# The shared expert's halves run beside routing and beside the scan, and the out projection shares the down product's accumulation

## Chip, cores and metric

The program runs on one core of a Trainium2 chip. The metric is the device time of one execution in microseconds (us), as the median of several runs. Engines are called PE or TensorE (matrix products), DVE or VectorE, ACT or ScalarE, POOL or GpSimd, and SP, which here only issues DMAs. Each has its own queue and works through it in order; they meet by semaphores.

## What is computed

T = 8192 rows (2 sequences of 4096) of H = 1024 values. Each row is normalised, a small state-space branch (D = 96 channels, N = 16 states) and a mixture of experts run on the normalised rows, and all is added up:

```python
xn = _layernorm(x)
x = x + attn(xn) + ffn(xn)
# attn: z = layer_norm(xn, w, b) @ in_proj.T      (1024 -> 96)
#       u = silu(conv3(z)); delta = softplus(...) * 0.001
#       state = exp(delta*A) * state + delta*B*u ; y = C . state + u*D
#       out = y @ out_proj.T + xn                 (96 -> 1024)
# ffn:  router: sigmoid scores, 4 of 8 groups, 8 of 32 experts, weights * 2.5
#       routed = sum over the 8 of w * (silu(x@Wg) * (x@Wu)) @ Wd   (inner 512)
#       shared = silu(x@Sg) * (x@Su) @ Sd                           (inner 1024)
```

## The kernel before

It has four stages, each a block in which all engines start together and end together.

**route_stage** (L64 to L533) takes 16 chunks of C = 512 rows, each J = 4 tiles of 128. `norms` on DVE makes `xn` for four tiles in one go, with the power -1/2 from POOL; POOL adds `bs = xt + xn`; SP stores xn and bs. PE turns xn (`transposes`, into `tp`) and multiplies it with the router's and the projection's weights (`project`, into `lg`). `route` on DVE picks the experts of a chunk and computes for each row and expert the slot in a table; slots and weights (`payload`) stay in SBUF for all rows. The 96 projected channels stay in SBUF as `zT`.

**scan_stage** (L536 to L922) takes the same 16 chunks. Channels times states make 1536 lines, in NG = 12 groups of 128. For each group PE spreads delta and delta*u (`spread_to`, four products into `rep_d` and `rep_u`), ACT takes the exponential (`dA`), DVE multiplies (`dBu`) and runs the recurrence (`hs`, L884), POOL multiplies with C (`hc`, L669) and PE collects (`collect`, into `yp`, a float32 product). `rep_d`, `rep_u` and `op` have two buffers each. Eight half tiles of the out projection (`out_half`, L758) run in groups 3 to 10 of the next chunk; DVE adds them to the base rows that SP has loaded (`add_half`, L871), and SP stores them as output.

**plan_stage** (L935 to L1054) counts the rows of each expert, lists the tiles, and meanwhile loads the first weights and gathers the first rows.

**expert_stage** (L1057 on) runs 656 tiles of 128 rows through one half expert of inner width 512 each: first SH * T / P = 128 tiles of the shared expert (two halves, 64 tiles each), then 528 of the routed experts. Every float32 operand is split into a high and a low part (type fp32r), and each product is three products:

```python
m(dst, hi, whi[:, cols], start=begin, stop=False)              # L1409
m(dst, hi, wlo[:, cols], start=False, stop=False)              # L1410
return m(dst, lo, whi[:, cols], start=False, stop=end)         # L1411
```

PE's order in a tile t is: gate (24 products, into `pg`), up (24, into `pu`), turning the rows of t+1 (8, into `tx`), the down product of t-1 (24, into `pd`), turning the activated tile (4, into `ta`, L1445). ACT makes the high parts and Silu, DVE the low parts (L1321 for weights, L1332, L1337), `av = pu * sg` (L1370) and the scaled result (L1344). POOL gathers the rows by table and adds results to the output by indirect DMAs. While the first 64 tiles run, POOL also writes the table of slots: eight indirect DMAs of 128 entries in each tile (`scatter`, L1200).

## Time and profile before

| | us |
|---|---|
| median of 3 runs | 13304.63 |
| lowest, highest | 13290.81, 13305.15 |
| profiled execution, device time | 13301.22 |
| its span in the trace | 13299.4 |
| TensorE busy in it | 12585.9 (95%) |
| VectorE, ScalarE, GpSimd busy | 4435.6, 2255.9, 2837.1 |

The span is what the trace covers; it lies 1.8 us under the device time of the same execution. A busy TensorE is not one at its peak: its ends are modelled, so a product's cost is read from one start to the next. The columns of a timeline row are start, duration, engine, line, operation, tile written <- tiles read, shape and count, and in brackets the idle time just before with what ended it.

### The profile page before, as it was taken

How to read it: one execution, taken by the hardware profiler on the slowest of the kernel's cores; microseconds unless marked ns; L12 is line 12 of the kernel's file. 1: busy time of each engine (PE TensorE's matmuls, PEld its weight loads, DVE VectorE, ACT ScalarE, POOL GpSimd, SP SyncE). 2: the span in 40 equal slices, each digit the busy share in tenths (PEclk: the TensorE clock that was granted, in tenths of full speed). 3: DMA queues.
4: the chain of work that ended last, by engine and by line, in shares of the span. 5: the costliest groups of instructions: out<-in, count | busy, mean ns of one | idle time of the engine just before them, and what ended most of it. 6: DMA issues, size and time to landing. Idle time of an engine off the chain costs nothing.

```text
span 13299.4 us, 218878 instructions
## 1 busy us (share of the span) xinstructions
PE 12585.9 (95%) x58520; PEld 10224.2 (77%) x58521; DVE 4435.6 (33%) x6772; ACT 2255.9 (17%) x3430; POOL 2837.1 (21%) x2929
## 2 busy tenths in 40 slices
PE   4377799999999999999999999999999999999998
PEld 3333488888888888888888888888888788888887
DVE  8887622222222222222332223223233323222222
ACT  1133211111111111111111112111112212111111
POOL 3222266621111111111111111111111111111111
PEclk7688899999999999999999999999999999999999
DMA  4312222232232332333332324323334434223322
GB/s 187 136 63 76 87 61 60 60 78 59 59 78 60 78 79 59 77 60 79 96 98 59 79 59 110 65 60 96 79 96 115 113 79 115 59 60 71 66 59 53
DMA packets 376393, 1057.82 MB, mean 80 GB/s; under 512 B 142082, under 2 KB 142530, under 8 KB 352552
## 3 DMA queue, kind: packets, MB, share of 16 engines
q0 software_dynamic: 205600, 689.56, 24.9%
q1 hardware_dynamic: 170760, 367.91, 7.5%
q14 instruction: 23, 0.19, 0.0%
q8 instruction: 10, 0.16, 0.0%
HBM read 608.87 MB, written 448.41 MB: 79 GB/s over the span
## 4 chain that ended last, share of the span: by engine, by line
PE 86%; DMA 1%; DVE 0%; issue 0%; ACT 0%; DVEq 0%; SPq 0%; ACTq 0%; POOL 0%; POOLq 0%
PE pg L1409 9%; PE pg L1411 9%; PE pd L1411 9%; PE pd L1410 9%; PE pg L1410 9%; PE pd L1409 9%; PE pu L1411 9%; PE pu L1410 9%; PE pu L1409 9%; PE tx L1404 4%; PE ta L1445 2%; DMA stage<-in_w_all 0%; DVE w_lo L1321 0%; ACT w_hi L1255 0%; DVEq L1054 0%
## 5 line engine op out<-in xcount | busy, mean ns | idle before, releaser
L1370 DVE TENSOR_TENSOR av<-pu,sg 128x512 f32<-128x512 f32 x656 | 453.8, 692 | 5681.0 <-PE pu L1411 5504.9
L1409 PE MATMUL pg<-w_hi,x_hi 128*128 128x512 f32 x5248 | 2113.7, 403 | 13.0 <-DVE x_lo L1332 13.0
L1409 PE MATMUL pd<-w_hi,a_hi 128*128 128x512 f32 x5248 | 2098.2, 400 | 8.1 <-DVEq L1356 8.0
L1411 PE MATMUL pd<-w_hi,a_lo 128*128 128x512 f32 x5248 | 2057.6, 392 | 0.0
L1411 PE MATMUL pg<-w_hi,x_lo 128*128 128x512 f32 x5248 | 2054.6, 392 | 0.0
L1410 PE MATMUL pd<-w_lo,a_hi 128*128 128x512 f32 x5248 | 2053.5, 391 | 0.0
L1410 PE MATMUL pg<-w_lo,x_hi 128*128 128x512 f32 x5248 | 2046.2, 390 | 0.0
L1411 PE MATMUL pu<-w_hi,x_lo 128*128 128x512 f32 x5248 | 2043.5, 389 | 0.0
L1409 PE MATMUL pu<-w_hi,x_hi 128*128 128x512 f32 x5248 | 2041.5, 389 | 0.0
L1410 PE MATMUL pu<-w_lo,x_hi 128*128 128x512 f32 x5248 | 2041.5, 389 | 0.0
L1214 POOL DMA_INDIRECT out_rows<-y,idx_s x656 | 1046.9, 1596 | 4266.2 <-DVE y L1344 4116.2
L1344 DVE TENSOR_SCALAR y<-pd,idx_s 128x512 f32<-128x512 f32 x1312 | 982.0, 751 | 1946.4 <-PE pd L1411 1901.4
L1259 ACT ACTIVATE x_hi<-tx 128x512 fp32r<-128x512 f32 x1314 | 720.9, 595 | 3437.5 <-PE tx L1404 3274.6
L1411 PEld LDWEIGHTS pg<-w_hi,x_lo 128*128 128x128 f32 x5248 | 985.6, 188 | 220.5
L1411 PEld LDWEIGHTS pd<-w_hi,a_lo 128*128 128x128 f32 x5248 | 985.4, 188 | 206.7
L1410 PEld LDWEIGHTS pu<-w_lo,x_hi 128*128 128x128 f32 x5248 | 985.3, 188 | 204.3
L1411 PEld LDWEIGHTS pu<-w_hi,x_lo 128*128 128x128 f32 x5248 | 985.3, 188 | 204.3
L1409 PEld LDWEIGHTS pu<-w_hi,x_hi 128*128 128x128 f32 x5248 | 985.3, 188 | 204.3
L1409 PEld LDWEIGHTS pd<-w_hi,a_hi 128*128 128x128 f32 x5248 | 987.9, 188 | 199.1 <-issue 9.5
L1409 PEld LDWEIGHTS pg<-w_hi,x_hi 128*128 128x128 f32 x5248 | 987.2, 188 | 199.6 <-DVE x_lo L1332 12.4
L1410 PEld LDWEIGHTS pg<-w_lo,x_hi 128*128 128x128 f32 x5248 | 989.6, 189 | 190.5
L1410 PEld LDWEIGHTS pd<-w_lo,a_hi 128*128 128x128 f32 x5248 | 988.3, 188 | 192.1
(227 smaller groups left out, 10228.4 us busy)
## 6 DMA issues: line engine op xcount, KB each, us to landing
stage<-in_w_all SPq DMA_DIRECT2D x186, 1024.0 KB, 9.3
xt<-in_x SPq DMA_DIRECT2D x16, 2048.0 KB, 12.9
xn_rows<-xn SPq DMA_DIRECT2D x16, 2048.0 KB, 6.7
base_rows<-bs SPq DMA_DIRECT2D x16, 2048.0 KB, 8.4
base<-base_rows SPq DMA_DIRECT2D x64, 512.0 KB, 5.6
out_rows<-base SPq DMA_DIRECT2D x64, 512.0 KB, 2.7
idx_g<-slot_table SPq DMA_DIRECT2D x658, 1.0 KB, 1.7
xraw<-xn_rows,idx_g POOLq DMA_INDIRECT x658
```

The lines of the kernel that those rows point to most:

```text
L1214: g.indirect_dma_start(out=out, out_offset=bass.IndirectOffsetOnAxis(ap=idx_s[q][:, 0:1], axis=0), in_=y[q][:], in_offset=None, compute_op ...
L1259: a.activation(x_hi[q][:, 4 * h:4 * h + 4], tx[h][:], ACT.Copy).then_inc(xh_ready, 1)
L1344: v.tensor_scalar(y[q][:, h * 512:(h + 1) * 512], pd[h][:], idx_s[q][:, 1:2].bitcast(F32), None, ALU.mult).then_inc(y_ready, 1)
L1370: v.tensor_tensor(av[:], pu[:], sg[:], ALU.mult).then_inc(av_ready, 1)
L1404: last = nc.tensor.transpose(tx[h][:, k], xraw[q][:, (4 * h + k) * P:(4 * h + k + 1) * P], ident[:])
L1409: m(dst, hi, whi[:, cols], start=begin, stop=False)
L1410: m(dst, hi, wlo[:, cols], start=False, stop=False)
L1411: return m(dst, lo, whi[:, cols], start=False, stop=end)
L1445: last = nc.tensor.transpose(ta[:, i], av[:, i * P:(i + 1) * P], ident[:])
```

## The change

The shared expert leaves the expert stage; that one now runs the 528 routed tiles alone, with its own first loads and gathers, which no longer lie in the plan stage.

In routing, the work goes tile by tile, no longer in chunks of four. The first half of the shared expert (6 weight chunks, each as high and low part in SBUF) runs on each tile. The rows that are turned for the router also feed the high and low parts, `sx_hi` and `sx_lo`, which are stored for the next stage. The result is added to the base rows (`summed`), which go to the output at once. `pd` is the pair `pg, pu`: the down product of t-1 overwrites the gate of t once Silu has read it. `route` is cut into four parts, one per tile. The projected channels go to memory (`z_d`) and come back in the scan. The scatters to the table are done here by POOL, eight per tile, the last 48 in the scan.

In the scan, the second half of the shared expert runs on the tiles of the chunk before. Its turned parts are loaded again by POOL's queue. PE's work of one group, a `slot`, stands after gate, after up and after down. The out projection of a half tile is accumulated onto its down product, and one addition puts both onto the output rows, which SP loads and stores. `rep_d` and `rep_u` have one buffer each, `hc` is split into two fp32r parts by ACT and DVE for the collection. Chunk 0 has no FFN; there its weights come in. The last chunk's FFN follows the scan.

The diff, cut to the order of the work (added lines; the removed ones are the loops described above; first the helpers, then GpSimd, TensorE and VectorE in routing, then TensorE and VectorE in the scan):

```diff
+def product(nc, dst, hi, lo, whi, wlo, cols, begin, end):
+    m = nc.tensor.matmul
+    m(dst, hi, whi[:, cols], start=begin, stop=False)
+    m(dst, hi, wlo[:, cols], start=False, stop=False)
+    return m(dst, lo, whi[:, cols], start=False, stop=end)
+def gate_or_up(nc, dst, xh, xl, w_hi, w_lo, base):
+    for k in range(KH):
+        n, c = base + k // 4, k % 4 * I
+        last = product(nc, dst, xh[:, k], xl[:, k], w_hi[n], w_lo[n], slice(c, c + I), k == 0, k == KH - 1)
+    return last
+def down_half(nc, dst, a_hi, a_lo, w_hi, w_lo, h, end=True):
+    for i in range(KI):
+        n, c = 4 + i // 2, i % 2 * H + h * 512
+        last = product(nc, dst, a_hi[:, i], a_lo[:, i], w_hi[n], w_lo[n], slice(c, c + 512), i == 0,
+                       end and i == KI - 1)
+    return last
...
+            def scatter(c, r, part):
+                wait_apart(pool, pool_passed, slots_ready, c + 1)
+                for n in range(part * K, part * K + K):
+                    g.indirect_dma_start(
+                        out=table, out_offset=bass.IndirectOffsetOnAxis(ap=slots[r][:, n:n + 1], axis=0),
+                        in_=payload[r][:, n], in_offset=None).then_inc(scattered[r], 16)
+            def chunk(c, r):
+                for k in range(J):
+                    if not ends(c, k, 1):
+                        base(*later(c, k, 1))
+                    if not ends(c, k, 2):
+                        cc, kk = later(c, k, 2)
+                        power(cc, kk)
+                        power2(cc, kk, r if k < 2 else 1 - r)
+                    if k and not (known(c, 0) or known(c, 1)):
+                        scatter(c - 2, r, k - 1)
+                    if not k and not (known(c, 0) or known(c, 1) or known(c, 2)):
+                        scatter(c - 3, 1 - r, 3)
...
+            def down(c, k):
+                t = c * J + k
+                pe.wait_ge(al_ready, t)
+                for h in range(2):
+                    if not ends(c, k, 0):
+                        pe.wait_ge((sg_ready, av_ready)[h], t + 1)
+                    down_half(nc, pd[h][:], a_hi, a_lo, w_hi, w_lo, h).then_inc(down_done, 1)
+            def chunk(c, r):
+                for k in range(J):
+                    t = c * J + k
+                    begun = not (known(c, 0) and k == 0)
+                    pe.wait_ge(xl_ready, t * 2 + 2)
+                    if not begun:
+                        pe.wait_ge(split_lo, 2)
+                    if not (known(c, 0) and k < 2):
+                        pe.wait_ge(y_ready, t * 2 - 3)
+                    gate_or_up(nc, pg[:], x_hi[k % 2], x_lo[k % 2], w_hi, w_lo, 0).then_inc(gate_done, 1)
+                    if not begun:
+                        pe.wait_ge(split_lo, 4)
+                    if not (known(c, 0) and k < 2):
+                        pe.wait_ge(y_ready, t * 2 - 2)
+                    gate_or_up(nc, pu[:], x_hi[k % 2], x_lo[k % 2], w_hi, w_lo, 2).then_inc(up_done, 1)
+                    if not ends(c, k, 1):
+                        turn_rows(*later(c, k, 1))
+                    if known(c, 0) and k == 1:
+                        pe.wait_ge(split_lo, 6)
+                    if begun:
+                        down(c, k)
+                    if not ends(c, k, 1):
+                        project(*later(c, k, 1), r if k < 3 else 1 - r)
+                    if k == 1 and not known(c, 0):
+                        z_turned(c - 1)
+                    if k == 3 and not known(c, 0):
+                        ranks(c - 1)
+                    pe.wait_ge(av_ready, t + 1)
+                    if not ends(c, k, 1):
+                        pe.wait_ge(xnT_ready, t * 2 + 3)
+                        pe.wait_ge(xl_ready, t * 2 + 3)
+                    for i in range(KI):
+                        last = nc.tensor.transpose(ta[:, i], sg[:, i * P:(i + 1) * P], ident[:])
+                    last.then_inc(ta_done, 1)
...
+            def chunk(c, r):
+                for k in range(J):
+                    t = c * J + k
+                    begun = not (known(c, 0) and k == 0)
+                    if begun:
+                        a_low(t - 1)
+                    if not ends(c, k, 2):
+                        norms(*later(c, k, 2), r if k < 2 else 1 - r)
+                    activated(t)
+                    if not ends(c, k, 1):
+                        x_low(*later(c, k, 1))
+                    if begun:
+                        summed(*later(c, k, -1))
+                    if k == 0 and not (known(c, 0) or known(c, 1)):
+                        route(c - 2, r, 3)
+                    if k < 3 and not known(c, 0):
+                        route(c - 1, 1 - r, k)
...
+            def slot(s, r, q):
+                if q + 1 < NG:
+                    spread_to(s, q + 1)
+                elif not last_of(s):
+                    spread_to(s + 1, 0)
+                if q:
+                    collect(s, r, q - 1)
...
+            def down_tile(t, chunk_done, j, y, end=False):
+                pe.wait_ge(al_ready, t + 1)
+                pe.wait_ge(y_ready, chunk_done)
+                for h in range(2):
+                    if not end:
+                        pe.wait_ge((sg_ready, av_ready)[h], t + 2)
+                    down_half(nc, pd[h][:], a_hi, a_lo, w_hi, w_lo, h, False)
+                    m(pd[h][:], y[:, j * P:(j + 1) * P], w_o[:, h * 512:(h + 1) * 512], start=False, stop=True)\
+                        .then_inc(down_done, 1)
+            def ffn_tile(mth, k, r, between):
+                t = mth * J + k
+                begun = not (known(mth, 0) and k < 2)
+                gate(t, k, begun)
+                between(0)
+                up(t, k, begun)
+                between(1)
+                if k:
+                    down_tile(t - 1, mth + 1, k - 1, yT[r])
+                elif not known(mth, 0):
+                    down_tile(t - 1, mth, J - 1, yT[1 - r])
+                between(2)
+                turn_activated(t)
...
+            def chunk(s, r):
+                for q in range(NG):
+                    k = q // 3
+                    t = s * J + (k - J)
+                    ffn = not known(s, 0)
+                    begun = ffn and not (known(s, 1) and k == 0)
+                    if q % 3 == 1 and ffn:
+                        activated(t)
+                    if q + 1 < NG:
+                        advance(s, r, q + 1)
+                    elif not last_of(s):
+                        if known(s, CPB - 1):
+                            dve.wait_ge(dA_free, CPB * NG)
+                            clear_state(2)
+                        advance(s + 1, 1 - r, 0)
+                    if not last_of(s):
+                        if q == 0:
+                            convolve(s + 1, 1 - r)
+                        if q == 5:
+                            bias_dt(s + 1)
+                        if 6 <= q < 10:
+                            softplus(s + 1, 1 - r, q - 6)
+                        if q == 10:
+                            lows(s + 1)
+                    if q == 1 and not known(s, 0):
+                        tail(s - 1, 1 - r)
+                    hc_low(s, q)
+                    if known(s, 0):
+                        weights_low(q)
+                    if q % 3 == 1 and begun:
+                        summed(t - 1, (k - 1) % J, 0)
+                    if q % 3 == 2 and begun:
+                        summed(t - 1, (k - 1) % J, 1)
+                    if q % 3 == 2 and ffn:
+                        a_low(t)
```

GpSimd's queue in routing, before: per chunk one power, four base sums, one power.

```order
23 L256 TENSOR_TENSOR rstd<-mv,minus_half 128x4
24 L258 ISA
25 L261 TENSOR_TENSOR bs<-xt,xn 128x1024
26 L258 REGISTER_ALU
27 L261 TENSOR_TENSOR bs<-xt,xn 128x1024
28 L258 REGISTER_ALU
29 L261 TENSOR_TENSOR bs<-xt,xn 128x1024
30 L258 REGISTER_ALU
31 L261 TENSOR_TENSOR bs<-xt,xn 128x1024
32 L264 TENSOR_TENSOR rs_0<-mv_0,minus_half 128x4
```

The same queue now, two tiles in the loop (`bases` is the base sum):

```order
104 L404 DMA slot_table<-payload,slots 262656x2 x8
105 L388 TENSOR_TENSOR bases<-xt,xn 128x1024
106 L391 REGISTER_ALU
107 L392 TENSOR_TENSOR rstd<-mv,minus_half 128x1
108 L396 TENSOR_TENSOR rs_1<-mv_1,minus_half 128x1
109 L404 DMA slot_table<-payload,slots 262656x2 x8
110 L388 TENSOR_TENSOR bases<-xt,xn 128x1024
```

Each tile has both powers, and eight scatters stand between them and the base sum.

TensorE's queue in the scan, before: one group, then a half of the out projection.

```order
317 L747 MATMUL rep_d<-d_hi,spread 128x512
318 L748 MATMUL rep_d<-d_lo,spread 128x512
319 L749 MATMUL rep_u<-du_hi,spread 128x512
320 L750 MATMUL rep_u<-du_lo,spread 128x512
321 L766 MATMUL yp<-hc,gather 96x512
322 L757 REGISTER_ALU
323 L758 MATMUL op<-w_o,yT 128x512
```

Now, from the end of a gate over one slot to the start of an up product (`tpg`, `tpu`, `tw_`, `tx_`: gate, up, weights and rows of the FFN in this stage):

```order
2374 L68 MATMUL tpg<-tw_hi,tx_lo 128x512
2375 L1210 ISA
2376 L1212 MATMUL rep_d<-d_hi,spread 128x512
2377 L1213 MATMUL rep_d<-d_lo,spread 128x512
2378 L1214 MATMUL rep_u<-du_hi,spread 128x512
2379 L1215 MATMUL rep_u<-du_lo,spread 128x512
2380 L1219 ISA
2381 L1222 MATMUL yp<-hc_hi,gather 96x512
2382 L1223 MATMUL yp<-hc_lo,gather 96x512
2383 L1256 REGISTER_ALU
2384 L66 MATMUL tpu<-tw_hi,tx_hi 128x512
```

A group's six products stand between blocks of 24, and the out projection has left this place.

VectorE's queue in routing now, the layer norm of one tile from its variance on, behind the low part of an activated tile and ahead of the product of gate and up (before, all four tiles of a chunk went through each of these steps together):

```order
156 L633 TENSOR_SCALAR mv<-mv 128x1
157 L634 REGISTER_ALU
158 L636 ISA
159 L637 REGISTER_ALU
160 L638 ISA
161 L639 TENSOR_SCALAR xn<-xt,mv,rstd 128x1024
162 L643 BN_STATS st<-xn 128x6 x2
163 L39 REGISTER_ALU
164 L645 BN_AGGR mv_0<-st 128x2
165 L56 REGISTER_ALU
166 L646 TENSOR_SCALAR mv_0<-mv_0 128x1
167 L673 TENSOR_TENSOR ssg<-spu,ssg 128x512
```

The product `ssg`, for which TensorE waits, stands behind the whole layer norm of a tile two ahead.

## Rows read from the trace of the kernel before

**Rows 1.** The page, the chain that ended last, shares of the span by engine.
```profile
PE 86%; DMA 1%; DVE 0%; issue 0%; ACT 0%; DVEq 0%; SPq 0%; ACTq 0%; POOL 0%; POOLq 0%
```
**Rows 2.** Busy by stage: length, PE, PEld, DVE, ACT, POOL, granted clock, DMA share, GB/s.
```profile
0.00:631.00 631.00, 260.22 (x1856) 235.35 (x1857) 564.12 (x1597) 90.49 (x196) 207.94 (x116) 0.70 0.44 166
631.00:1554.00 923.00, 681.67 (x1552) 317.03 (x1552) 711.85 (x1020) 312.44 (x422) 252.78 (x201) 0.83 0.19 73
1554.00:1593.00 39.00, 1.94 (x8) 1.57 (x8) 15.43 (x39) 9.56 (x7) 10.34 (x12) 0.50 0.53 202
1593.00:3862.00 2269.00, 2266.79 (x10730) 1883.74 (x10731) 559.84 (x775) 320.85 (x524) 873.75 (x1016) 1.00 0.29 64
3862.00:13262.00 9400.00, 9375.30 (x44376) 7786.55 (x44374) 2584.39 (x3345) 1522.52 (x2283) 1492.30 (x1586) 1.00 0.34 78
```
**Rows 3.** Timeline of the expert stage, a shared tile and the first routed gate.
```profile
2700.95 1.03 PE L1404 MATMUL tx<-ident,xraw 128*128 128x128 f32 x8
2701.21 0.69 DVE L1370 TENSOR_TENSOR av<-pu,sg 128x512 f32<-128x512 f32 x1 [9.28 <-PE pu L1411]
...
2713.21 0.39 PE L1409 MATMUL pu<-w_hi,x_hi 128*128 128x512 f32 x1
...
2718.66 1.03 PE L1404 MATMUL tx<-ident,xraw 128*128 128x128 f32 x8
...
3861.62 0.48 PE L1409 MATMUL pg<-w_hi,x_hi 128*128 128x512 f32 x1
```
**Rows 4.** Timeline of routing: layer norm, base sums, router's product, second part of routing.
```profile
27.57 7.06 DVE L421 TENSOR_SCALAR xn<-xt,mv,rstd 128x1024 f32<-128x1024 f32 x4 [1.17 <-POOL rstd L256]
28.47 10.71 POOL L261 TENSOR_TENSOR bs<-xt,xn 128x1024 f32<-128x1024 f32 x4 [0.93 <-DVE xn L421]
...
314.29 1.01 POOL L256 TENSOR_TENSOR rstd<-mv,minus_half 128x4 f32<-128x4 f32 x1 [22.99 <-DVE mv L415]
...
327.75 2.05 PE L340 MATMUL lg<-wcat,xnT 128*128 128x128 f32 x16 [0.74 <-ACT xnT L283]
...
332.29 0.09 DVE L463 MATCH_VALUE_LOAD gi<-g,gs 128x8 f32 x1
...
340.59 1.22 DVE L493 TENSOR_REDUCE w<-prod 128x32 f32<-128x1024 f32 x1
```
**Rows 5.** Timeline of the expert stage, scatters and a VectorE pass beside them.
```profile
2715.77 0.97 POOL L1200 DMA_INDIRECT slot_table<-payload_cur,slot_cur  x1 [0.30 <-issue]
2716.75 2.29 DVE L1321 TENSOR_TENSOR w_lo<-stage,w_hi 128x2048 fp32r<-128x2048 f32 x1 [7.50 <-ACT w_hi L1255]
2717.04 2.84 POOL L1200 DMA_INDIRECT slot_table<-payload_cur,slot_cur  x1 [0.30 <-issue]
```
**Rows 6.** Timeline of the scan.
```profile
671.14 1.28 DVE L884 TENSOR_TENSOR_SCAN hs<-dA,state,dBu 128x512 f32<-128x512 f32 x1
...
1308.74 0.77 PE L747 MATMUL rep_d<-d_hi,spread 96*128 96x512 f32 x1 [3.68 <-DVE dBu L880]
1309.30 0.63 PE L748 MATMUL rep_d<-d_lo,spread 96*128 96x512 f32 x1
1309.73 0.63 PE L749 MATMUL rep_u<-du_hi,spread 96*128 96x512 f32 x1
...
1320.31 1.28 ACT L712 ACT_TABLE_LOAD   x1
...
1322.81 1.02 PE L736 MATMUL op<-u,w_C 96*128 96x512 f32 x2
...
1323.89 0.39 PE L748 MATMUL rep_d<-d_lo,spread 96*128 96x512 f32 x1
```
**Rows 7.** Start of the expert stage; then the page's DMA issues (KB each, us to landing).
```profile
1580.61 7.31 ACT L1255 ACTIVATE w_hi<-stage 128x2048 fp32r<-128x2048 f32 x4 [57.82 <-PEq L943]
...
1593.37 0.80 PE L1409 MATMUL pg<-w_hi,x_hi 128*128 128x512 f32 x1 [10.80 <-DVE x_lo L1332]
...
stage<-in_w_all SPq DMA_DIRECT2D x186, 1024.0 KB, 9.3
```

More of the change, by code:

```diff
@@ L183, in route_stage, with chunks, known, ends @@
         block = ctx.enter_context(nc.Block())
+        def chunks(eng, chunk):
+            chunk(0, 0)
+            chunk(1, 1)
+            with eng.Fori(1, NC // 2 - 1) as i:
+                for r in range(2):
+                    chunk(i * 2 + r, r)
+            chunk(NC - 2, 0)
+            chunk(NC - 1, 1)
+        def known(c, n):
+            return isinstance(c, int) and c == n
+        def ends(c, k, d):
+            return isinstance(c, int) and c * J + k + d >= NT
         @block.sync
@@ new lines, in _ @@
+            for k in range(2):
+                power(0, k)
+                power2(0, k, 0)
+            base(0, 0)
+            pool.wait_ge(fills, FILLS)
+            chunk(0, 0)
+            chunk(1, 1)
+            chunk(2, 0)
+            chunk(3, 1)
+            with pool.Fori(2, NC // 2 - 1) as i:
+                for r in range(2):
+                    chunk(i * 2 + r, r)
+            chunk(NC - 2, 0)
+            chunk(NC - 1, 1)
+            scatter(NC - 3, 1, 3)
+            for part in range(J // 2):
+                scatter(NC - 2, 0, part)
@@ L311, in _ @@
+            for q in range(NCH):
+                act.wait_ge(staged[q % 2], q // 2 * 16 + 16)
+                a.activation(w_hi[q][:], stage[q % 2], ACT.Copy).then_inc(split_hi, 1)
+                if q == 1:
+                    x_high(0, 0)
+            chunks(act, chunk)
+            a_high(NT - 1)
+            z_row(NC - 1, 1)
         @block.tensor
@@ L379, in _ @@
+            turn_rows(0, 0)
+            project(0, 0, 0)
+            chunks(pe, chunk)
+            down(NC, 0)
+            z_turned(NC - 1)
+            ranks(NC - 1)
         @block.vector
@@ L553, in sem, with sems @@
             return ctx.enter_context(nc.semaphore(name))
+        def sems(name, n):
+            return [sem(f"{name}{i}") for i in range(n)]
+        w_hi = ring("tw_hi", [P, WC], F32R, NCH)
+        w_lo = ring("tw_lo", [P, WC], F32R, NCH)
+        x_hi = ring("tx_hi", [P, KH, P], F32R)
+        x_lo = ring("tx_lo", [P, KH, P], F32R)
+        sg = sb("tsg", [P, I])
+        a_hi = sb("ta_hi", [P, KI, P], F32R)
+        a_lo = sb("ta_lo", [P, KI, P], F32R)
+        sums = sb("sums", [P, 2, H])
+        bs = [sums[:, q] for q in range(2)]
+        ident = sb("tident", [P, P])
         cw = sb("cw", [D, 3])
@@ L671, in _ @@
+            chunks(pool, chunk, ((4, NC),))
+            for k in range(2):
+                t = NT - J + k
+                pool.wait_ge(up_done, t + 1)
+                load_x(t + 2, k)
+            pool.wait_ge(scattered, LEFT * 16)
         @block.scalar
@@ L1424, in down @@
                 for h in range(2):
[L1425 to L1429 removed]
+                    down_half(nc, pd[h][:], a_hi, a_lo, w_hi, w_lo, h).then_inc(down_done, 1)
             def tile(t, q):
```

1441 lines of the change are left out of this document (825 added, 616 removed).

## The prediction

> **What bounds the kernel now.** I read the chain that ended last first, then the stages. The chain is 86% TensorE, and waits for anything else are 1% or less [rows 1]. The stages say where that holds [rows 2]: routing (0 to 631) and scan (631 to 1554) keep TensorE busy for 260 of 631 and 682 of 923 us at a mean clock of 0.70 and 0.83, with VectorE at 564 and 712. The expert stage runs it without a hole at full clock: 2267 of 2269 us for the 128 shared tiles (1593 to 3862), 9375 of 9400 for the 528 routed ones. The last 37 us hold no work. So a tile in the expert stage costs what TensorE needs for it: 17.71 us from one turning of rows to the next [rows 3], of which 72 products are 72 x 0.227 = 16.35 (24 of them lie between 2713.21 and 2718.66, 5.45 us). Whoever moves 128 tiles under stages in which TensorE has holes saves the holes. The question is how much of 17.71 each tile costs there.
>
> **What goes.** The 128 shared tiles lie between the first gate product at 1593.37 [rows 7] and the first routed one at 3861.62 [rows 3]: 2268 us. From there the routed part is unchanged in its instructions; it lasts 13299.4 - 3861.6 = 9438 us, its closing loops included. Its first tile now starts without a predecessor's down product (5.5 us less) and at the low clock (some 4 more), so I keep 9436. The wait that SP gets there, for a gather issued two tiles ago, costs nothing: that gather had to land before the tile's own products.
>
> **The routing stage.** TensorE now has, per tile, what the expert tile has (17.71, the turned rows are shared with the router), and the router's product, 2.05 with its modelled end [rows 4]. That is 19.7 to 19.8. What must fit beside it:
> - VectorE had 564 us for 64 tiles, 8.8 each. The FFN adds six passes over 128x512 (av, two x_lo, a_lo, two sums) at 0.69 [rows 3]: 12.9 of 19.8. But it is not even: the second part of routing takes 8.3 (332.29 to 340.59) and falls in one tile of four. There it is 8.3 + 4.1 + the layer norm of one tile. Unbatched, that is two passes of statistics at 1.2, xn 0.9 (its start at 27.57 to Pool's at 28.47, when Pool is idle), Pool's power 1.0, and an estimated 2 for small operations and hand-overs: 6.3. Sum 18.7, and the chain has to come round before the second half of the down product, which waits for av. I take 1 us per chunk for it.
> - GpSimd gets a ring of its own. Per tile it does power, second power, eight scatters that stood in the expert stage before, and the base sum. VectorE's layer norm stands between the two powers. Scatters start 1.27 apart (2715.77, 2717.04) [rows 5], so 0.8 + 8 x 1.27 = 11.0; base 10.71 / 4 = 2.7; two powers 2.0; VectorE between them 3.1. Ring: 18.8. It fits under 19.8 by 1 us only.
> - The base rows no longer go to memory and come back; out, turned rows and rows are stored instead, about 2.5 MB per tile of 20 us, 125 GB/s. The stage moved 166 GB/s before [rows 2]. SP waits in order (base, xn, x_lo, sums); each is a tile old when needed. I cost it at nothing; if the stores came later than one tile, VectorE's xn would wait for them.
>
> So a tile costs 19.8 if all fits; I take 20.3, for the 1 us per chunk and some port trouble on Pool, and hold 22.5 as the upper bound (first rival). The start: six weight chunks pass two staging buffers, each 9.3 to land [rows 7], 1.8 for w_hi (7.31 / 4) [rows 7] and 2.3 for w_lo [rows 5]; three rounds of 13.4 after a first arrival near 24 (an estimate) end at 64, VectorE then owes the layer norm of tile 2 with Pool's base before it, and the gate of tile 1 starts at 76. 62 tiles of 20.3 lead to the last gate at 1335. Behind it: its own products 11, down product of the tile before 5.5, turning and its two parts 2.5, 18 of routing left to VectorE, and about 8 for sums, stores and the barrier: 45. **Routing ends at 1380**, against 631.
>
> **The scan stage.** A tile's blocks of 24 products now alternate with slots of the scan. Per tile: 16.35 + 0.35 for turning, three slots of six products of the same kind (four spreads and the collection as two parts), 18 x 0.227 = 4.1, two halves of the out projection accumulated onto the down product, and one of the four projections of a chunk. Those three are plain float32, two passes each; two passes and one single product lie between 1322.81 and 1323.89, 1.08, so 0.85 for one [rows 6]. Sum 23.4, with changes of mode 23.5: 94 us per chunk. Beside it VectorE has 712 / 16 = 44.5 per chunk, twelve low parts of hc at 0.69 and sixteen passes of the FFN at 0.69: 64. ScalarE 312 / 16 = 19.5, twelve high parts and eight FFN passes at an estimated 0.6 (w_hi's 2048 columns take 1.8, [rows 7]), and table loads, since each tile's Silu stands between exponentials: 2 x 1.28 [rows 6] per tile, about 42. Both fit. Single spread buffers make each slot wait for the exponential and product of the slot before, but a block of 5.45 lies between: after a gate, Silu with its load, the exponential with its load and the high part need about 4.5, the recurrence, state and low part end near 6.1, and TensorE comes for them at 5.45 + 1.4 + 0.9 = 7.7. With the convolution (2.7 more), the logarithms with their load and the last softplus part in front of the low part, it is late by about 1.1, 2.2 and 0.8. So 4 us per chunk, 98; bounds 94 and 106. The stage then is: 40 until the first recurrence (671 as before, [rows 6]) and 3 for new constants; chunk 0 without FFN, (923 - 40) / 16 = 55 plus twelve half w_lo at 1.15 and low parts at 0.69, 77; 15 x 98 = 1470; four tiles alone, (16.7 + 1.7 + 0.5) x 4 = 76; the last down product and store 14. Sum 1680. **Scan ends at 3060**, with 3 for the barrier.
>
> **The start of the expert stage.** The plan is as long as before, 27 us (1554 to 1580.61, [rows 2, 7]). Before, weights and rows of the first tiles came in beside it, and the first gate was 12.8 us later (1593.37). Now they are asked for only after it. The bound below is those 12.8; above, two landings of 9.3 and the last w_hi, w_lo and x_lo on top, 25. I take 21. First gate at 3060 + 3 + 27 + 21 = 3111.
>
> **Sum.** 3111 + 9436 = 12,547 span. The profiled execution took 13,301.2 for a span of 13,299.4, and the median is 13,304.6, 3.4 above it, so I forecast **12,550**, 5.7% below.
>
> **A rule against it.** One scatter of 0.97 took 2.84 when VectorE's w_lo, a pass with two SBUF inputs, started just ahead of it [rows 5]; xn took 7.06 / 4 = 1.8 where Pool's base ran, 0.9 alone [rows 4]. The Trainium skill (SBUF — State Buffer, Who interferes with whom) says that such VectorE passes and a GpSimd instruction that reads SBUF exclude each other for a whole instruction. By that rule, with which these rows agree, each meeting costs the rest of the other's pass, and routing ends nearer to rival 1; by the 1.27 of the undisturbed scatters it ends where the sum has it.
>
> Routing's one-hot products now meet the scatters, which in the kernel before they never did.
>
> **Rivals.**
> 1. *Pool's ring sets the routing pace.* If two of eight scatters per tile meet such a pass, each 1.87 longer, the ring is 18.8 + 3.7 = 22.5: 2.2 more for 62 tiles, 136 us, **12,690**. For it: slack of only 1 us. Against it: most of VectorE's routing passes take 0.2 to 0.4, so a meeting costs less than with w_lo.
> 2. *The scan's chain is not hidden.* If at each of two slots per tile one table load and one exponential show (2 x 2 us, 60 tiles) and another 1 us at the third, 5 x 60 = 300: **12,850**. For it: the ScalarE queue is strict and carries both chains. Against it: 7.7 us stand against 6.1.
> 3. *TensorE stays at its low level, slower than before.* After a hole of 3.68 us at 1308.74 the products at 1309.30 and 1309.73 start 0.43 apart, against 0.227 [rows 3, 6]: the 1.2 and the 2.4 GHz level. If the waits between blocks held both stages low, 124 tiles would cost 72 x 0.2 = 14.4 more each, 1790, **14,340**. It decides from 42% of the tiles on (750 / 1790). Against it: the holes I expect are 1 to 2 us among 20 of work. The Trainium skill (TensorE: Matmul & The Clock Gate, A second HAM failure mode: psum-queue depth-cycling) tells of short idles between groups that bring the gate down; the two float32 stages before show low clocks only around longer holes.
> 4. *Nothing shows.* All waits fit, 19.8 and 94: 31 and 60 less, **12,460**.
>
> **How the numbers follow.** Forecast with rival 4 as its lower edge (12,460 to 12,640): 0.69. Rival 1: 0.17, up to 12,780. Rival 2: 0.10. Rival 3: 0.03. Something that eats the gain just so: 0.01. Leaving out rivals 2 and 3 the range is 12,455 to 12,780; it takes in the bounds of the expert start and most of the ends of both tile prices. Faster by over 0.2% (27 us, about what a measurement of this kernel can tell from no change): 0.96; within: 0.01; slower: 0.03.
>
> **What would show it.** The first routed gate product near 3111; routing's end near 1380 and scan's near 3060; TensorE's clock at 1.0 in both; turnings of rows 20.3 apart in routing and 24.5 in the scan; Pool's idle before its base sums small but not nil. If Pool is never idle and TensorE waits for x_lo or av, rival 1 holds. If TensorE waits for hc's low part or the exponential in most slots, rival 2. I would be wrong altogether if a store or a load on SP's queue came late in each tile, which no row of the kernel before can show.

## The result, and the profile after

| | before | after |
|---|---|---|
| median, us | 13297.72 (4 runs, 13289.22 to 13305.15) | 12448.01 (4 runs, 12445.38 to 12459.0) |
| ratio | | 0.9363, 95% interval 0.9349 to 0.9377 |
| span of the profiled execution | 13299.4 | 12447.2 |

The kernel is 6.4% faster. The forecast was 12,550 and the range 12,455 to 12,780: right in direction and nearly in size, but the median lies 7 us below the range. What happened is nearest to rival 4, "nothing shows", and it came out below the 12,460 that I gave it. So the question is which terms of the sum were too dear, and whether the cover that made them cheap is wide or narrow.

First the chain that ended last, from the page of the kernel after, answering [rows 1], and then the busy times by stage, answering [rows 2] (length, PE, PEld, DVE, ACT, POOL, granted clock, DMA share, GB/s): routing, scan, plan and start, routed tiles, and at the end the regular part of routing and of the scan by themselves.

```profile
PE 74%; DMA 1%; DVE 0%; issue 0%; ACT 0%; DVEq 0%; SPq 0%; ACTq 0%; POOL 0%; POOLq 0%
```

The shares do not add up to 100%, because the profile follows this chain back only to 3000.6, where the first weights of the routed experts are loaded. It says nothing of routing and scan; for these the busy times count.

```profile
0.00:1354.00 1354.00, 1284.93 (x6720) 1085.08 (x6721) 850.37 (x2065) 274.97 (x456) 685.70 (x669) 0.99 0.38 135
1354.00:2979.00 1625.00, 1555.74 (x6400) 1171.01 (x6400) 893.34 (x1344) 600.79 (x827) 389.66 (x382) 0.96 0.27 89
2979.00:3020.00 41.00, 1.94 (x8) 1.57 (x8) 15.96 (x36) 8.61 (x6) 2.96 (x7) 0.52 0.49 193
3020.00:12447.00 9427.00, 9364.04 (x44352) 7782.73 (x44352) 2577.36 (x3339) 1522.93 (x2282) 1491.48 (x1583) 1.00 0.34 77
86.14:1316.93 1230.79, 1208.20 (x6359) 1020.49 (x6358) 789.59 (x1928) 248.97 (x426) 640.63 (x614) 1.00 0.37 131
1519.36:2850.00 1330.64, 1330.64 (x5600) 1015.36 (x5600) 758.12 (x1146) 514.43 (x711) 315.26 (x316) 1.00 0.27 91
```

TensorE was busy for 260 of 631 us in routing and now is for 1285 of 1354; in the scan for 682 of 923 and now for 1556 of 1625. In the last row busy and length are the same number: over 1331 us of the scan the profile shows no idle time of TensorE. Both stages now run at a granted clock of 1.00 in their regular parts, against means of 0.70 and 0.83 before.

The places that divide the time, each row by itself (start, duration, engine, line, operation; in brackets the idle time before and what ended it): the gates of tiles 1, 2 and 63 in routing; the scan's first DMA, first recurrence and first gate; the plan's first instruction; the first routed gate.

```profile
64.85 0.78 PE L66 MATMUL spg<-sw_hi,sx_hi 128*128 128x512 f32 x1
...
86.14 0.48 PE L66 MATMUL spg<-sw_hi,sx_hi 128*128 128x512 f32 x1
...
1316.93 0.48 PE L66 MATMUL spg<-sw_hi,sx_hi 128*128 128x512 f32 x1
...
1368.88 0.33 SPq L975 DMA_DIRECT2D cw<-in_convw  x1
...
1405.90 1.28 DVE L1378 TENSOR_TENSOR_SCAN hs<-dA,state,dBu 128x512 f32<-128x512 f32 x1
...
1472.22 0.79 PE L66 MATMUL tpg<-tw_hi,tx_hi 128*128 128x512 f32 x1 [3.25 <-DVE tw_lo L1398]
...
2982.39 0.16 POOL L1536 IOTA reg_i<- 128x32 int32 x1 [56.18 <-ACTq L1496]
...
3020.11 0.80 PE L66 MATMUL pg<-w_hi,x_hi 128*128 128x512 f32 x1 [10.63 <-DVEq L1889]
```

Against the terms of the sum (the gate of tile 60, the first of the four that follow the scan, stands at 2895.24):

| term | forecast | measured | difference |
|---|---|---|---|
| gate of tile 1 | 76 | 64.9 | -11 |
| 62 tiles of routing | 20.3 each, to 1335 | 20.2 each, to 1316.9 | -7 |
| last gate to the scan's start | 45 | 52.0 | +7 |
| scan, to the first recurrence | 43 | 37.0 | -6 |
| chunk 0 | 77 | 66.3 | -11 |
| 15 chunks of the scan | 98 each | 94.9 each | -47 |
| last four tiles, store, barrier | 93 | 87.2 | -6 |
| plan and start | 48 | 37.7 | -10 |
| first routed gate to the end | 9436 | 9427.1 | -9 |
| sum | 12,547 | 12,447.2 | -100 |

Eight of the nine differences have one sign, so they add up instead of cancelling. The one term that was too cheap is the end of routing: GpSimd's last scatter ends at 1360.7, 43.8 us behind the last gate.

### The profile page after: what moved, and what is told of

Read it like the earlier page. It is cut to its first block, busy times and chain, and to the rows that moved or that the text cites. A ratio compares the mean times of both kernels' runs of the same rounds, so it can differ in the third digit from the quotient of the medians.

```text
span 12447.2 us, 204853 instructions
## 1 busy us (share of the span) xinstructions
PE 12206.7 (98%) x57480; PEld 10040.4 (81%) x57481; DVE 4337.0 (35%) x6781; ACT 2407.3 (19%) x3571; POOL 2569.8 (21%) x2640
## 3 DMA queue, kind: packets, MB, share of 16 engines
q8 instruction: 88, 1.44, 0.1%
## 4 chain that ended last, share of the span: by engine, by line
PE 74%; DMA 1%; DVE 0%; issue 0%; ACT 0%; DVEq 0%; SPq 0%; ACTq 0%; POOL 0%; POOLq 0%
PE pg L66 8%; PE pg L68 8%; PE pd L68 8%; PE pg L67 8%; PE pd L67 8%; PE pd L66 8%; PE pu L68 8%; PE pu L67 8%; PE pu L66 8%; PE tx L1925 4%; PE ta L1950 2%; DMA stage<-in_w_all 1%; DVE w_lo L1844 0%; ACT w_hi L1778 0%; DVEq L1583 0%
## 5 line engine op out<-in xcount | busy, mean ns | idle before, releaser
L66 PE MATMUL pg<-w_hi,x_hi 128*128 128x512 f32 x4224 | 1702.2, 403 | 11.9 <-DVEq L1889 10.6
L66 PE MATMUL pd<-w_hi,a_hi 128*128 128x512 f32 x4224 | 1689.3, 400 | 7.7 <-DVEq L1879 7.7
L68 PE MATMUL pg<-w_hi,x_lo 128*128 128x512 f32 x4224 | 1653.8, 392 | 0.0
L68 PE MATMUL pd<-w_hi,a_lo 128*128 128x512 f32 x4224 | 1652.2, 391 | 0.0
L67 PE MATMUL pd<-w_lo,a_hi 128*128 128x512 f32 x4224 | 1648.8, 390 | 0.0
L67 PE MATMUL pg<-w_lo,x_hi 128*128 128x512 f32 x4224 | 1647.1, 390 | 0.0
L68 PE MATMUL pu<-w_hi,x_lo 128*128 128x512 f32 x4224 | 1645.1, 389 | 0.0
L66 PE MATMUL pu<-w_hi,x_hi 128*128 128x512 f32 x4224 | 1643.1, 389 | 0.0
L67 PE MATMUL pu<-w_lo,x_hi 128*128 128x512 f32 x4224 | 1643.1, 389 | 0.0
L1733 POOL DMA_INDIRECT out_rows<-y,idx_s x528 | 842.3, 1595 | 3664.3 <-DVE y L1867 3564.9
```

The costliest lines, as they stand in the source:

```text
L1733: g.indirect_dma_start(out=out, out_offset=bass.IndirectOffsetOnAxis(ap=idx_s[q][:, 0:1], axis=0), in_=y[q][:], in_offset=None, compute_op ...
```

## The experiments

Times of single runs are the median of one; the kernel before stood at 13,297.8 to 13,299.8 beside them.

**How much room have the other engines?** If the blocks of products only just cover the rest, thinner blocks change little; if there is room, the time falls until the next bound.

`route_thin` and `scan_thin`, in one stage each:

```diff
 def product(nc, dst, hi, lo, whi, wlo, cols, begin, end):
     m = nc.tensor.matmul
+    if THIN[0]:
+        return m(dst, hi, whi[:, cols], start=begin, stop=end)
     m(dst, hi, whi[:, cols], start=begin, stop=False)
```

> In the routing stage each product of the shared half is one product instead of three (the two with a low part are left out, so that half is less exact); all waits and all other engines stay. TensorE then has 48 x 0.227 = 10.9 us less per tile, 8.6 to 10.2. My theory: GpSimd's ring is the next bound, and it is 16.6 us as the changed kernel's trace shows it (two powers 0.6 each, VectorE's layer norm 3.0, eight scatters 10.1, base sum 2.4), so a chunk of four tiles takes 67 instead of 80.7 and routing ends some 210 us earlier: about 12,240. The prediction's ring of 18.8 gives 75 per chunk, 85 us earlier: 12,360. If neither ring nor VectorE holds, a chunk takes VectorE's 52 busy us, 440 earlier: 12,010.

> The same in the scan stage: one product instead of three in each block of the shared half there. TensorE has 43.6 us less per chunk, 51.6 instead of 95.2. My theory: the recurrence's chain and VectorE had much room behind the blocks; with 54 busy us per chunk on VectorE and 63 for the twelve slots of chunk 0, a chunk takes about 65, 15 x 30 = 450 us less: about 12,000. Rival 2 of the prediction (the chain is not hidden, and the blocks only just cover it) lets a chunk fall by no more than 10: 12,300 or more.

Measured: 12,261.7 and 11,988.3. The longest group of TensorE's waits in the regular part of each (total us, how many, longest), first routing, then scan:

```profile
PE spu L70 <- DVE ssg L678: 243.4, 58, 7.7
```

```profile
PE yp L1227 <- DVE hc_lo L1393: 116.8, 58, 3.3
```

In routing there are 93.5 us more in 29 places, for the low part of the activated tile (VectorE, L673), ahead of the next turning of rows.

In `route_thin` a chunk takes 71.4 us ((1074.3 - 217.4) / 12) instead of 80.7: between the 67 that GpSimd's ring of 16.6 gives and the 75 of the forecast's 18.8. The starts of its power operations show why: 17.6, 20.5, 16.8 and 16.6 apart. Two tiles of four run at the ring of 16.6, in the two others VectorE comes to the layer norm late, with one or two parts of routing ahead of it. In `scan_thin` a chunk takes 67.8 us ((2422.6 - 1541.2) / 13). So the scan's chain and VectorE need at most 68 of the 95 us that TensorE needs, and rival 2 is wrong by far. Where TensorE's blocks are thin, and it waits for up to 7.7 us, the granted clock is lower too: 0.78 over this part of routing and 0.94 in the scan. That is rival 3's mechanism, with holes that the full blocks don't leave.

**GpSimd's ring**, measured from the other side:

```diff
                         in_=payload[r][:, n], in_offset=None).then_inc(scattered[r], 16)
+                    g.indirect_dma_start(
+                        out=spare, out_offset=bass.IndirectOffsetOnAxis(ap=slots[r][:, n:n + 1], axis=0),
+                        in_=payload[r][:, n], in_offset=None).then_inc(scattered[r], 16)
```

> Each of the eight scatters of a tile is followed by a second one of the same entries to a spare table that nobody reads: GpSimd's ring gets 8 x 1.27 = 10.1 us longer, nothing else changes. With the ring of 16.6 that the trace shows it is 26.7 and sets the pace: 60 tiles x (26.7 - 20.2) = 390 more, about 12,840. With the 18.8 of the prediction it is 28.9: 520 more, about 12,970. If GpSimd's scatters are off the path altogether (more room than 10 us), nothing changes.

Measured: 12,866.8, 419 more than the changed kernel. A tile takes 27.2 us ((1604.4 - 299.2) / 48), as the ring of 16.6 + 10.1 says. The ring itself, in the changed kernel's timeline of GpSimd, one tile from power to power:

```profile
920.98 0.57 POOL L392 TENSOR_TENSOR rstd<-mv,minus_half 128x1 f32<-128x1 f32 x1
924.57 0.55 POOL L396 TENSOR_TENSOR rs<-mv,minus_half 128x1 f32<-128x1 f32 x1 [3.02 <-DVE mv L646]
925.32 1.04 POOL L404 DMA_INDIRECT slot_table<-payload,slots  x1 [0.20 <-issue]
...
934.25 0.96 POOL L404 DMA_INDIRECT slot_table<-payload,slots  x1 [0.30 <-issue]
935.23 2.40 POOL L388 TENSOR_TENSOR bases<-xt,xn 128x1024 f32<-128x1024 f32 x1
937.59 0.57 POOL L392 TENSOR_TENSOR rstd<-mv,minus_half 128x1 f32<-128x1 f32 x1
```

16.6 from 920.98 to 937.59. The forecast's 18.8 was too dear in three places. It took eight scatters as 11.0; from the first to the base sum they take 9.9. It took a power as 1.0, from one over four columns [rows 4]; over one column it is 0.57. It took the base sum as 2.7, and it is 2.4. Against a tile of 20.2 us the ring leaves 3.6 us of room, not 1.

**The scan's chain**, longer by a known amount:

```diff
+                for e in range(1):              # low_plus2: range(2)
+                    v.tensor_tensor(extra[...], hc[:], hc_hi[q % 2][:], ALU.subtract)
                 v.tensor_tensor(hc_lo[q % 2][:], hc[:], hc_hi[q % 2][:], ALU.subtract).then_inc(hl_ready, 1)
```

> In the scan each low part of hc is computed twice, first into a spare tile: VectorE's part of each slot's chain, just ahead of the low part that the collection waits for, is 0.69 us longer. The prediction had the chain late already, by 4 us per chunk, so 0.69 in at least three slots of a chunk would show: 2 us x 15 = 31 more, 12,480. By the trace of the changed kernel TensorE never waits, with 0.5 to 2 us of room in the tightest slots: under 6 us more, 12,450.

> Two spare passes instead of one, 1.38 us per slot. By the trace's room (0.5 us in the slots behind which softplus stands, 1.0 in those after an up product, 2 and more elsewhere) four slots of a chunk are late, by 0.9, 0.9, 0.4 and 0.4: 2.6 x 15 = 39 more, about 12,485. If low_plus1 shows nothing and this one nothing, the room is over 1.4 us everywhere. If the chain were as tight as predicted: 12 x 0.7 and more, over 12,550.

Measured: 12,459.6 and 12,493.9, 12 and 46 more. From the scan's first DMA to the plan's first sum (DVE L1547 in the changed kernel) it is 1623.1 and 1651.6 us against 1614.2. Of the 9 and 37 us more, 5.5 and 11.9 lie ahead of the first gate, in the start and chunk 0; the chunks with FFN take 3.5 and 25.6 more, and with one extra pass no wait of TensorE is listed between 1500 and 2950, with two this:

```profile
PE yp L1223 <- DVE hc_lo L1391: 15.4, 28, 2.7
```

So 0.69 us more per slot is hidden but for 0.2 us in a chunk (3.5 / 15), and 1.38 is late in two slots of a chunk (28 waits in 15 chunks, 15.4 us; what the other 10 of the 25.6 are, the list of waits doesn't show). The three tightest slots of a chunk are those for which the forecast had the chain late. In the changed kernel's timeline they are these (VectorE's low part, then TensorE's product that comes for it): first the slot with the logarithm and softplus's first part, then the one with softplus's last part, then the one with the convolution, the last from the start of its spread on.

```profile
2103.76 0.69 DVE L1388 TENSOR_TENSOR hc_lo<-hc,hc_hi 128x512 fp32r<-128x512 f32 x1
2104.93 0.39 PE L1222 MATMUL yp<-hc_hi,gather 128*96 128x512 f32 x1
...
2126.82 0.68 DVE L1388 TENSOR_TENSOR hc_lo<-hc,hc_hi 128x512 fp32r<-128x512 f32 x1
2128.54 0.40 PE L1222 MATMUL yp<-hc_hi,gather 128*96 128x512 f32 x1
...
2143.79 0.39 PE L1212 MATMUL rep_d<-d_hi,spread 96*128 96x512 f32 x1
2146.68 1.28 DVE L1378 TENSOR_TENSOR_SCAN hs<-dA,state,dBu 128x512 f32<-128x512 f32 x1 [1.07 <-ACT dA L1117]
2148.19 0.48 DVE L1332 TENSOR_SCALAR temps<-zs,cw 96x512 f32<-96x512 f32 x1
2150.16 0.68 DVE L1388 TENSOR_TENSOR hc_lo<-hc,hc_hi 128x512 fp32r<-128x512 f32 x1
2151.59 0.39 PE L1222 MATMUL yp<-hc_hi,gather 128*96 128x512 f32 x1
```

The low part is ready at 2104.45, 2127.50 and 2150.84, and TensorE comes 0.5, 1.0 and 0.75 us later. The forecast had the chain 2.2, 0.8 and 1.1 late in these slots. In all other slots the room is 2 us or more in the median.

**The holes that are left in routing.** The changed kernel's TensorE waits in routing, from the start of its regular part:

```profile
PE spu L66 <- DVE ssg L673: 22.5, 23, 1.4
```

12 of the 23, 1.0 to 1.4 us each and 15.5 us together, sit in the tile behind routing's second part; the other 11, 7.0 us together, in the tile before. The second part's last operation looks like this beside GpSimd's base sum:

```profile
978.89 3.83 DVE L740 TENSOR_TENSOR prod<-oh,score 128x256 f32<-128x256 f32 x4
...
979.02 2.41 POOL L388 TENSOR_TENSOR bases<-xt,xn 128x1024 f32<-128x1024 f32 x1
```

The four products take 3.83 us where the base sum starts among them and 1.42 where not: 2.41 more, the base sum's own length. `prod_late` moves them one tile on:

```diff
                 if part == 1:
 ...
-                    for j in range(J):
-                        last = v.tensor_tensor(prod[:, j * K:(j + 1) * K], oh[:, j * K:(j + 1) * K], ...)
-                    s(last)
                 if part == 2:
+                    for j in range(J):
+                        last = v.tensor_tensor(prod[:, j * K:(j + 1) * K], oh[:, j * K:(j + 1) * K], ...)
+                    s(last)
```

> The four products of one-hot and score at the end of routing's second part are moved to the head of the third, from a tile in which VectorE is 1.4 us late with the product of gate and up to one in which it has room. My theory: TensorE's only holes in routing are these (22.5 us in 23 places, 1.4 in one tile of four), so one in each chunk goes: 15 x 1.2 = 18 us less. The rival: VectorE meets GpSimd's base sum in another place and the hole only moves, no change.

Measured: 12,424.67 (5 runs, 12,424.0 to 12,426.2), ratio to the kernel before 0.9344 (0.9330 to 0.9357), 23 us under the changed kernel. Its waits and its regular part of routing:

```profile
PE spu L66 <- DVE ssg L673: 5.7, 6, 1.0
```

```profile
85.07:1293.76 1208.69, 1203.01 (x6360) 1021.57 (x6358) 758.27 (x1926) 248.97 (x426) 639.98 (x613) 1.00 0.38 134
```

VectorE does the same work in 758.3 busy us instead of 789.6. In the new place the four products take 1.42 to 1.47 us in every chunk: they don't meet the base sum. A tile takes 19.8 us on average, what TensorE has to do.

**The plan.** Loads of the first routed expert's weights back in the plan stage: on SP's queue ahead of the list (`plan_sp`), on ScalarE's (`plan_act`), on SP's behind the list together with `prod_late` (`tail`); all three take expert 0 as the first tile's.

```diff
+            for q in range(NCH):
+                sp.dma_start(stage[q][:], w_all[q]).then_inc(staged[q], 16)
             sp.wait_ge(done, PLAN_STEPS)
             for n in range(5):
                 sp.dma_start(plan_d[n].rearrange("(p f) -> p f", p=P), rows_i[n][:]).then_inc(listed, 16)
```

> The six weight chunks of the first routed expert are loaded in the plan stage, on SP's queue ahead of the list of tiles, as the kernel before did with the shared expert's (expert 0 is taken for granted as the first). My theory: the list's trip to memory and back then waits behind 6 MB again: plan 27 us instead of 13.4, and the first gate 13 to 16 us behind it instead of 24.3, so the first gate moves by less than 4 us from 37.7 behind the scan's end. The rival, the prediction's reading that the plan takes 27 whatever is loaded, can't be: it was 13.4. If the loads do not delay the list, 13 + 13 = 26: 11 us earlier.

> The same loads on ScalarE's queue, which is idle in the plan. If the list only waited in SP's own queue, plan 13.4 and first gate 13 behind it: 11 us earlier than in the changed kernel. If it waits for the 16 engines that all queues share, the plan takes 20 or more, and 5 us or less are gained.

> prod_late and plan_act together: 18 + 11 = 29 us less than the changed kernel if both theories hold, about 12,420; with the list delayed, 18 + 5.

> prod_late, and the six loads of the first expert's weights issued on SP's queue in the plan stage right behind the loads of the list, so that the list waits for none of them. My theory, that the list's trip is delayed by whatever megabytes are under way and not by its queue: the trip stays at 4 us, the loads start 5 us earlier than in prod_late, and the first gate comes 33 us behind the plan's start instead of 37.7. Rival: the loads take as long as ever (8 us each, bound by memory), first gate at 37.

Measured: 12,452.9, 12,446.4, 12,423.6 (5 runs, 12,419.7 to 12,428.6) and 12,431.8. None is clearly faster than its counterpart without the loads. `tail` is 7 us above `prod_late`, but that lies behind the first routed gate: from there to the end `tail` takes 9436.8 us and `prod_late` 9429.3, with the same instructions, and this stage alone differs by up to 11 us between the profiled kernels. The 0.2 to 3.6 us that the loads gain in front of it are lost in that. The list of tiles on its way to memory and back, store and first load, in the changed kernel and in `plan_act`:

```profile
2988.71 2.22 SPq L1527 DMA_DIRECT2D tile_list<-row  x5
2992.75 0.24 SPq L1530 DMA_DIRECT2D starts<-tile_list  x1
```

```profile
2986.18 2.32 SPq L1527 DMA_DIRECT2D tile_list<-row  x5
2998.83 0.24 SPq L1530 DMA_DIRECT2D starts<-tile_list  x1
```

4.0 us without weights under way, 12.7 with 6 MB on another queue, and 14.0 in `plan_sp` (2986.98 to 3000.93) on its own. In `tail` the list is quick (4.3), but now the numbers of the first rows wait behind the weights, SP's issue and GpSimd's gather that waits for the landing:

```profile
2972.51 1.47 SPq L1707 DMA_DIRECT2D idx_g<-slot_table  x2
```

```profile
2985.56 1.04 POOL L1750 DMA_INDIRECT xraw<-xn_rows,idx_g  x1 [13.36 <-DMA idx_g<-slot_table]
```

From the plan's first sum to the first gate it is 37.1 us in the changed kernel, 35.3 in `plan_sp`, 34.0 in `plan_act`, 33.3 in `both`, 36.7 in `tail`; `prod_late`, without such loads, is at 36.9. Of the 11 us that an undelayed list would have given, at most 4 come: the delay changes its victim, and most of it stays.

**One change too many.** `best` puts routing's fourth part into the fourth tile, which has no part of its own, and takes the loads of `tail`. Its expectation calls it `tail` with this move, but its source is the changed kernel with the move and the loads: the products that `prod_late` had moved stand in their old place again. So it has to be compared with the changed kernel, and against `prod_late` it differs in two things.

```diff
-                    if k == 0 and not (known(c, 0) or known(c, 1)):
-                        route(c - 2, r, 3)
-                    if k < 3 and not known(c, 0):
+                    if not known(c, 0):
                         route(c - 1, 1 - r, k)
```

> tail, and routing's fourth part moved from the head of the next chunk's first tile, where it stood beside the first part (10 us of VectorE in one tile), to the fourth tile, which had none. TensorE's last regular hole in routing, 1.2 us in the second tile of every other chunk (7 x 1.2), goes: 8 us less than tail, about 12,412 together. The rival: the low part of the activated tile comes late instead, and nothing is gained.

Measured: 12,464.6 (5 runs, 12,459.5 to 12,472.0), ratio 0.9369 (0.9357 to 0.9382): 17 more than the changed kernel, which is little more than these kernels differ from run to run, and 40 more than `prod_late`. The old product with the score, L740, no longer meets the base sum (1.42 to 1.44 in each chunk). But the product of one-hot and slot, L762, which stands in the moved part, meets it in 9 chunks of 16, against 3 in the changed kernel:

```profile
620.50 4.30 DVE L762 TENSOR_TENSOR prod<-oh,slotrow 128x256 f32<-128x256 f32 x4
```

```profile
622.11 2.39 POOL L388 TENSOR_TENSOR bases<-xt,xn 128x1024 f32<-128x1024 f32 x1
```

It is not alone. Counting VectorE's passes of routing that take over 1.2 us longer than the same pass does in the median, all of them beside a base sum, there are 25 in the changed kernel (52.7 us more), 7 in `prod_late` (19.1) and 28 in `best` (74.6), where seven of the passes that mask the scores (L723) are among them, at 2.8 to 3.0 us instead of 0.3. TensorE waits 33.6 us for the product of gate and up in `best`, in 18 places, against 22.5 in the changed kernel. 12.1 of these 33.6 come once in two chunks, behind the end of VectorE's loop: there the queue now has the moved part and then, without anything that the profile names, 2.8 and 1.5 us of idle time at 371.4 and 374.9. How much of the loss is due to the one and how much to the other no run separates. What holds is that spreading the parts evenly by their own lengths did not pay.

## Why the prediction was nearly right, and where it was not

**What bounds the kernel, and what goes.** Right. The 128 shared tiles took 17.72 us each; routing, scan and these tiles together now end 1429 us behind the place where the two stages alone ended before (2982.4 against 1553.6), 11.2 per tile. The routed part is 9427 us. My 9436 lies in what this stage shows from one profile to another: in the twelve profiled kernels that have it alone it is 9427.1 to 9438.1 long, and 9437.8 in the kernel before. So 9 of the 100 us say nothing about the sum.

**Routing: 20.3 per tile.** Right in sum (20.2), partly for a wrong reason. VectorE is late by about 1 us in some tiles, as I took it, mostly behind the second part of routing. That the tile then came out at 20.2 is in part luck: I had put the trouble of the two engines with each other on GpSimd's side, and it is VectorE's products that are held up by the base sum. Without that, in `prod_late`, the tile is 19.8. GpSimd, which I thought the narrow place, had 3.6 us of room: the step that failed is the ring's 18.8, too dear by 1.1 for the scatters, 0.9 for two powers whose price came from a batch of four columns, and 0.3 for the base sum. Rival 1 had a chance of 0.17 on a slack that was more than three times as wide.

**The start of routing: 76.** Too dear by 11. Three rounds of 13.4 us through two staging buffers, each with a landing of 9.3, were to end at 64. The last four loads are issued at 31.2, 33.4, 40.2 and 43.3, and the high parts that wait for them start 4.7 to 6.8 us later; the last low part ends at 54.3, and the gate of tile 1 stands at 64.9. The 9.3 was a landing beside the work of the expert stage.

**Chunk 0: 77.** Too dear by 11. I added 22 us of new VectorE work to 55, the mean of the sixteen chunks before. But chunk 0 was no such chunk: it had no additions of the out projection, eight of 0.69, which start in the next one. Its twelve slots in the kernel before:

```profile
671.14:721.13 49.99, 34.67 (x80) 16.62 (x79) 41.23 (x54) 18.25 (x26) 14.73 (x12) 0.77 0.00 0
```

50.0 long, with VectorE busy for 41.2. Now the twelve slots (1405.90 to 1468.94) take 63.0, with 57.6 of them busy. So about 5 of the 11 us are the wrong chunk taken as the measure; and of 16.4 us of additional busy time only 13.0 show, since the rest fell into holes. To the first gate it is 3.3 us more.

**The scan's chunks: 94 and 4 of waits.** This is the step that failed with the most in it, 47 of the 100 us. The 94 was 1.2 too low (TensorE alone needs 95.2 in a full chunk). The 4 us of waits per chunk, 1.1, 2.2 and 0.8 for the low part, don't exist: the chain of these three slots was mis-sized. From the start of the spread, medians over the chunks:

| slot with | low part ready, forecast | measured | TensorE comes, forecast | measured |
|---|---|---|---|---|
| the convolution | 8.8 | 7.0 | 7.7 | 7.8 |
| the logarithm and softplus's first part | 9.9 | 8.2 | 7.7 | 8.6 |
| softplus's last part | 8.5 | 6.7 | 7.7 | 7.8 |

The convolution does stand in the chain with its whole length, between the recurrence and the low part (2148.19 to 2150.16 in the rows above). But it takes 2.0 us there and not 2.7, and the chain without it about 5.1 and not 6.1. In the logarithm's slot TensorE also comes 0.9 us later than I took it, because one of the four projections stands ahead of the block. `low_plus1` shows that 0.69 us more in each slot costs 0.2 us in a chunk, and `low_plus2` where the room ends.

**Plan and start: 27 + 21.** The plan's 27 us were not its own work: VectorE was done after 6.7, and the list's way to memory and back took 14.2 us (1560.27 to 1574.51) beside the weights (`plan_sp` brings it back: 14.0 instead of 4.0). Now the plan takes 13.4 (2982.4 to 2995.8) and the start 24.3, 3 more than I took. The step that failed is "the plan is as long as before", after the loads beside it had gone.

**The rule against the change.** The Trainium skill (SBUF — State Buffer, Who interferes with whom) says that a VectorE pass with two SBUF inputs and a GpSimd instruction that reads SBUF exclude each other. The runs agree, with 2.41 us more in a row of 1.42. But it fell elsewhere than I feared: of 464 scatters in routing 15 took over 1.5 us, less than one in a chunk. The payer is VectorE, whose one-hot products stand beside the base sum, while the base sum keeps its 2.35 to 2.42 us in all 64 tiles. "Routing's one-hot products now meet the scatters" was the wrong pair.

**TensorE's clock.** Rival 3 (0.03) needed 42% of the tiles at the low level; both stages are at 1.00. The waits of 1.4 us between blocks of 5.45 do not bring it down, while the thin blocks of `route_thin` do.

**The range.** It promised to take in the bounds of the unknown costs, but its lower end was one case, "nothing shows", with the terms of start, chunk 0 and plan as they were. With these three as they came (11, 11 and 10 less) it would have been 12,428.

## What to carry to other kernels

When work moves under another stage, price the stage by what its engines do, not by its length: part of new work falls into holes, a mean over chunks is not the price of the first chunk, a batch's price is no single's price, and a stage's length may be made by a transfer that the change takes away. An independent upper and lower bound for every term, start and end included, matters as much as the rivals: many small terms that err the same way add up to more than the range. And before balancing engines by the lengths of their parts, look at which passes run beside the other engine's SBUF reads; the same products cost 1.4 or 3.8 us. Last, read the difference of two kernels from their sources before explaining a difference in time: `best` was not the kernel that its expectation describes.

## What the runs showed of the hardware

- A small transfer that is issued behind 6 MB takes 11.9 to 14 us for its round trip instead of 4, and it helps little to use another queue: 12.7 (`plan_act`) and 11.9 (`both`) with the weights on ScalarE's, 14.0 on SP's own. The Trainium skill (DMA: Bandwidth & Descriptors, Queues, rings and completion order) says that each DMA engine takes turns between its queues packet by packet. In `plan_act` the list did not slip through by this, or gained one or two microseconds; with the weights behind it, in `tail`, it took 4.3. By what the bytes under way hold it up no run here shows.
- A VectorE pass that meets GpSimd's base sum (128x1024, 2.4 us) ends 0.3 us after it. Four products of 1.42 us together take 3.83 where it starts beside the first (2.4 more). They take 4.30 where it starts 0.6 us after the fourth, at 622.11 in `best` (2.9 more); that product, at 621.50, would by its usual 0.42 have been over by then. The base sum itself is not longer for it.
- TensorE's granted clock is 1.00 over 1331 us of changing shapes and types, float32 turnings, float32 projections and split products, with no wait of TensorE listed among them; in the regular part of routing it is 1.00 too, with 23 waits of at most 1.4 us. A float32 product of 128x512, the out projection between two blocks, occupies it for 0.87 us there (from 2109.00 to 2110.10, with one split product of 0.227 in between), against 0.227 for one of the three products of a split one:

```profile
2109.00 1.02 PE L1276 MATMUL tpg<-w_o,yT 96*128 96x512 f32 x2
2109.46 0.80 PE L66 MATMUL tpu<-tw_hi,ta_hi 128*128 128x512 f32 x1
2110.10 0.40 PE L67 MATMUL tpu<-tw_lo,ta_hi 128*128 128x512 f32 x1
```
